# A selective-scan layer and a routed expert layer on one core: drives and scans by halves of a slot, states summed by accumulating transposes, and the gate by rows

## What is computed

```python
x_ssm, x_gate = split(x @ in_proj_w.T + in_proj_b)
x_conv = silu(conv1d(x_ssm) + conv_b)            # 4 taps, per channel
B, C   = split(x_conv @ bc_w.T + bc_b)           # 16 states each
dt     = softplus(x_conv @ dt_w.T + dt_b)
h = h * exp(dt * A) + dt * B * x_conv            # per channel and state, along the tokens
y = (sum over states of h * C + x_conv * D) * silu(x_gate)
out = y @ out_w.T + out_b + x                    # then the layer norm
```

## Time and profile before

| | |
|---|---|
| median of 3 runs | 1368.25 us (1363.77 to 1369.27) |
| the profiled execution | 1371.27 us |
| its span | 1369.4 us |
| stage 1, from the first drive to the last scan | 37.8 to 608.5 us |
| busy over the span | PE 85%, DVE 77%, ACT 66%, POOL 58% |

### The profile page before, as it was taken

The page is one execution under the profiler, slowest core; times in us unless marked ns, Lnnn a source line. Parts: engine busy times, 40 slices in busy tenths (PEclk is TensorE's granted clock), DMA queues, the critical chain, the costliest instruction groups (busy, mean ns, idle before and its releaser), DMA issues. The chain is left out here.

```text
span 1369.4 us, 18063 instructions
## 1 busy us (share of the span) xinstructions
PE 1168.3 (85%) x5138; PEld 802.5 (59%) x5138; DVE 1061.2 (77%) x1558; ACT 899.0 (66%) x1551; POOL 792.0 (58%) x566
## 2 busy tenths in 40 slices
PE   7879697988969797765799999999999999999940
PEld 3324252434334343324588888888888888888840
DVE  2999899999989999994777777777777777777744
ACT  4775849485856768425467777767767776767734
POOL 0457568888878888897643444444444444444342
PEclk9899999999999999887899999999999999999985
DMA  2543434545443545336676655566565655565537
GB/s 97 206 155 123 171 107 172 172 149 180 146 167 149 205 150 170 136 104 241 233 216 161 161 144 136 149 158 160 158 160 159 160 139 138 147 163 159 159 38 246
DMA packets 69258, 217.18 MB, mean 159 GB/s; under 512 B 7520, under 2 KB 43232, under 8 KB 56288
## 3 DMA queue, kind: packets, MB, share of 16 engines
q1 hardware_dynamic: 29664, 167.42, 34.0%
q0 software_dynamic: 26880, 36.72, 15.7%
q10 hardware_dynamic: 12672, 12.58, 2.8%
HBM read 165.54 MB, written 51.15 MB: 158 GB/s over the span
## 5 line engine op out<-in xcount | busy, mean ns | idle before, releaser
L641 PE MATMUL p_y<-read,small 128*128 128x512 f32 x512 | 260.4, 644 | 84.2 <-POOL read L1175 84.2
L1041 DVE TENSOR_TENSOR_SCAN state<-decay,p_bu 128x1024 f32<-128x1024 f32 x128 | 292.5, 2285 | 19.3 <-ACT decay L822 10.2
L1497 POOL DMA_INDIRECT total<-o_v,tok x144 | 266.0, 1847 | 45.4 <-issue 45.3
L641 PEld LDWEIGHTS p_y<-read,small 128*128 128x128 f32 x512 | 100.8, 205 | 226.9 <-POOL read L1175 123.3
L1495 POOL TENSOR_TENSOR scrap<-neg_half 128x1 f32<-128x1 f32 x36 | 13.0, 362 | 319.8 <-ACT o_v L1404 317.3
L822 ACT ACTIVATE decay<-dt,scan_rate 128x511 f32<-128x511 f32 x256 | 165.2, 713 | 20.6 <-DVE state L1041 20.2
L1175 POOL TENSOR_TENSOR read<-state,bc 128x1024 f32<-128x1024 f32 x64 | 150.2, 2353 | 34.5 <-DVE p_bu L1032 17.6
L505 ACT ACTIVATE gate_v<-p_g,bias 128x512 f32<-128x512 f32 x144 | 98.5, 684 | 103.0 <-PE p_up L495 96.8
L1217 POOL DMA_INDIRECT queues<-rows,index x128 | 134.4, 1050 | 31.7 <-issue 28.9
L1391 ACT ACTIVATE ah<-a_v 128x512 fp32r<-128x512 f32 x144 | 91.2, 633 | 93.0 <-DVE a_v L519 89.3
L1175 POOL TENSOR_TENSOR read<-state,first_wh 128x1024 f32<-128x1024 f32 x32 | 75.4, 2357 | 65.3 <-DVE p_bu L1032 51.7
(11 more groups left out here) (222 smaller groups left out, 3014.7 us busy)
## 6 DMA issues: line engine op xcount, KB each, us to landing
bc<-bc_rows SPq DMA_DIRECT2D x32, 1024.0 KB, 4.9
first_raw<-in_w_experts SPq DMA_DIRECT2D x19, 1668.0 KB
raw_w<-in_w_experts SPq DMA_DIRECT2D x18, 1668.0 KB
first_wh<-bc_rows SPq DMA_DIRECT2D x16, 1024.0 KB
first_wl<-bc_rows SPq DMA_DIRECT2D x16, 1024.0 KB
first_rows<-queues SPq DMA_DIRECT2D x19, 544.0 KB
xq<-queues SPq DMA_DIRECT2D x18, 544.0 KB
queues<-pad SPq DMA_DIRECT2D x9, 544.0 KB
```

Of the source, the lines that this page charges most:

```text
L641: mm = pe.matmul(p_y[h][:, :], ident[:, :], read[:, t % 4, h, :], start=False, stop=(t == SLOTS - 1))
L1041: dve.tensor_tensor_scan(flat(state[t % 4][:, :, :]), flat(decay[t % AHEAD][:, :, :]), p_bu[:, :], 0.0, ALU.mult, ALU.add).then_inc(s_stat ...
L1497: pool.indirect_dma_start(total, bass.IndirectOffsetOnAxis(ap=tok[t.p][:, a:a + 1], axis=0), o_v[t.p][:, a, :], None, compute_op=ALU.add). ...
```

## The change

1. **Halves.** Drive and scan of a slot become two instructions each, of 128x512. The order on DVE is drive(half 0), drive(half 1), what else the slot has, scan(half 0), scan(half 1). A half waits for its own half alone: the drive for the scan of the same half in the slot before, the scan for its drive and its decay. ACT and POOL wait for both halves, counted twice.
2. **Sums by transposes.** `sum_states` becomes 8 transposes of 128x128 (the product as stationary operand, the identity moving) that accumulate in `p_y`, so that `p_y` has tokens on its partitions. The start with `x_conv * D` becomes 8 matmuls of 128x128.
3. **The gate by rows.** `project_gate` makes the gate with tokens on the partitions: 8 products of 128x256 and 4 with the bias in three bf16 parts. The parts are made once, at the start (`spread_gate_bias`, `in_parts`). ACT copies without a bias.
4. **Turning back.** The gated `y_rows` is turned by 8 transposes (`turn_rows`, t = 3 on PE) into two new blocks of `p_bank`, which ACT copies into `y` (`take_turned`, first on ACT's list at t = 3). `project_out` waits for both copies.

```diff
-        return (["tr0", "tr1", "rt"] * d + ["in0", "in1"] * a + ["o0", "o1"] * c + ["cnt"] * d + ["cv0", "cv1"] * a
+        return (["tr0", "tr1", "rt"] * d + ["in0", "in1"] * a + ["yt0", "yt1", "o0", "o1"] * c + ["cnt"] * d + ["cv0", "cv1"] * a
...
+        def project_gate(r, b):
+
+            bank, done = block(r, f"in{HALVES + b}")
+            if r.like == Round.FIRST and b == 0:
+                pe.wait_ge(s_set_dve, 4)
+            for i in range(2):
+                to, at = bank[:, i * D:(i + 1) * D], (2 * b + i) * P
+                product(to, lambda k: xt[:, k, at:at + P], lambda k: w[:, k, IN + D:IN + 2 * D], stop=False)
+                mm = pe.matmul(to, ones[0:3, :], gate_parts[0:3, :], start=False, stop=True)
+            mm.then_inc(done, 1)
...
+            def of_rows(h, b):
+                return p_y[b // 2][:, b % 2 * D + h * P:b % 2 * D + (h + 1) * P]
+
             if t == 0:
                 after(pe, s_y, s.n)
                 for h in range(HALVES):
-                    pe.matmul(p_y[h][:, :], skip_w[:, h, :], xc[s.p][:, h, :], start=True, stop=False)
+                    for b in range(TT):
+                        pe.matmul(of_rows(h, b), xc[s.p][:, h, b * P:(b + 1) * P], skip_w[:, h, :],
+                                  start=(h == 0 and b % 2 == 0), stop=False, skip_group_check=True)
             pe.wait_ge(s_read, n + 1)
             for h in range(HALVES):
-                mm = pe.matmul(p_y[h][:, :], ident[:, :], read[:, t % 4, h, :], start=False, stop=(t == SLOTS - 1))
+                for b in range(TT):
+                    mm = pe.matmul(of_rows(h, b), read[:, t % 4, h, b * P:(b + 1) * P], ident[:, :], is_transpose=True,
+                                   start=False, stop=(t == SLOTS - 1), skip_group_check=True)
             mm.then_inc(s_added, 1)
+
+        def turn_rows(r, h):
+
+            bank, done = block(r, f"yt{h}")
+            if h == 0:
+                pe.wait_ge(s_y, r.s.at(-1).n + 1)
+            for b in range(TT):
+                mm = pe.transpose(bank[:, b * P:(b + 1) * P], y_rows[:, b, h * P:(h + 1) * P], ident[:, :])
+            mm.then_inc(done, 1)
 
         def project_out(r, b):
 
             bank, done = block(r, f"o{b}")
             s = r.s.at(-1)
-            if b == 0:
-                pe.wait_ge(s_y, s.n + 1)
+            for h in range(HALVES):
+                src, n = r.block(f"yt{h}")
+                pe.wait_ge(bank_read[src], n)
...
+        def take_turned(r, h):
+
+            bank, done = full(act, r, f"yt{h}")
+            act.activation(y[:, h, :], bank[:, :], ACT.Copy).then_inc(done, 1)
...
+        def weigh_inputs(s, t, h):
+
+            if t == 0 and h == 0:
                 dve.wait_ge(s_u, s.n + 1)
-            arrived(dve, s, t)
-            after(dve, s_state, SLOTS * s.n + t)
-            dve.tensor_tensor(p_bu[:, :].rearrange("p (a b) -> p a b", a=2), p_u[:, :].rearrange("p (a b) -> p a b", a=2),
-                              of_state(t, 0), ALU.mult).then_inc(s_bu, 1)
-
-        def scan(s, t):
-
-            n = SLOTS * s.n + t
-            dve.wait_ge(s_bu, n + 1)
-            dve.wait_ge(s_decay, 2 * n + 2)
-            after(dve, s_read, n - 3)
-            dve.tensor_tensor_scan(flat(state[t % 4][:, :, :]), flat(decay[t % AHEAD][:, :, :]), p_bu[:, :],
+            if h == 0:
+                arrived(dve, s, t)
+            after(dve, s_state, halves_done(s, t - 2) + h + 1)
+            dve.tensor_tensor(p_bu[:, h * LEN:(h + 1) * LEN], p_u[:, h * LEN:(h + 1) * LEN], row_of(t, 0), ALU.mult)\
+               .then_inc(s_bu, 1)
+
+        def scan(s, t, h):
+
+            dve.wait_ge(s_bu, halves_done(s, t - 1) + h + 1)
+            dve.wait_ge(s_decay, halves_done(s, t - 1) + h + 1)
+            if h == 0:
+                after(dve, s_read, SLOTS * s.n + t - 3)
+            dve.tensor_tensor_scan(state[t % 4][:, h, :], decay[t % AHEAD][:, h, :], p_bu[:, h * LEN:(h + 1) * LEN],
                                    0.0, ALU.mult, ALU.add).then_inc(s_state, 1)
...
             for h in range(HALVES):
-                last = dve.tensor_tensor(y[:, h, :], p_y[h][:, :], sg[s.p][:, h, :], ALU.mult)
+                last = dve.tensor_tensor(flat(y_rows[:, 2 * h:2 * h + 2, :]), p_y[h][:, :], sg[s.p][:, h, :], ALU.mult)
             last.then_inc(s_y, 1)
```

More of the change, by code:

```diff
@@ L264, in build @@
     y = sb("y", HALVES, LEN, at=one)
+    y_rows = sb("y_rows", TT, D, at=one)
+    gate_parts = sb("gate_parts", D, dt=BF16, at=one)
     z = sb("z", TT, D, at=one)
@@ L690, in count @@
             mm.then_inc(done, 1)
+        spread_gate_bias()
         for r in rounds(pe):
@@ L707, in pe_stage1 @@
                 if r.c and t == 3:
+                    turn_rows(r, 0)
+                    turn_rows(r, 1)
                     project_out(r, 0)
@@ L727, in pe_stage1 @@
                 if r.a and t in (10, 11):
-                    project(r, t - 8)
+                    project_gate(r, t - 10)
                 if t >= 2 and r.b:
@@ L761, in store_in @@
                 after(act, s_y, s.n - 1)
-            to = xpad[:, m, TAPS - 1:TAPS - 1 + LEN] if m < 2 else sg[s.p][:, m - 2, :]
-            act.activation(to, bank[:, :], ACT.Identity, bias=b_in[:, m:m + 1]).then_inc(done, 1)
+            if m < 2:
+                last = act.activation(xpad[:, m, TAPS - 1:TAPS - 1 + LEN], bank[:, :], ACT.Identity, bias=b_in[:, m:m + 1])
+            else:
+                last = act.activation(sg[s.p][:, m - 2, :], bank[:, :], ACT.Copy)
+            last.then_inc(done, 1)
         def store_conv(r, h):
@@ L816, in decays @@
         def decays(s, t):
-            after(act, s_state, SLOTS * s.n + t - AHEAD + 1)
+            after(act, s_state, halves_done(s, t - AHEAD))
             if t == 0:
@@ L879, in act_stage1 @@
             for t in range(SLOTS):
+                if r.c and t == 3:
+                    take_turned(r, 0)
+                    take_turned(r, 1)
                 if r.d and t == 3:
@@ L963, in dve_setup, with in_parts @@
         dve.tensor_reduce(b_bc2[:, :], b_bc[:, :], AX.X, ALU.add).then_inc(s_set_dve, 1)
+        def in_parts(to):
+            steps.then(dve.memset(to[:, :], 0.0))
+            for i in range(3):
+                steps.then(dve.tensor_copy(b_part[:, :], b_rest[:, :]))
+                if i < 2:
+                    steps.then(dve.tensor_tensor(b_rest[:, :], b_rest[:, :], b_part[:, :], ALU.subtract))
+                steps.then(dve.scalar_tensor_tensor(to[:, :], b_part[:, :], ident[:, i:i + 1], to[:, :], ALU.mult, ALU.add))
+        dve.wait_ge(s_gate_bias, 1)
+        steps.then(dve.tensor_copy(b_rest[:, :], p_bu[:, 0:D]))
+        in_parts(gate_parts)
         dve.wait_ge(s_const, SETUP)
         steps.then(dve.tensor_tensor(b_rest[:, :], b_out[:, :], ln_b[:, :], ALU.subtract))
[L967 to L973, removed]
+        in_parts(b_parts)
     def dve_setup_rest(dve):
@@ L1121, in dve_stage1 @@
                 if r.b:
-                    weigh_inputs(r, t)
+                    for h in range(HALVES):
+                        weigh_inputs(r.s, t, h)
                 if r.c and t == 2:
@@ L1162, in dve_stage1 @@
                 if r.b:
-                    scan(r.s, t)
+                    for h in range(HALVES):
+                        scan(r.s, t, h)
         return plan_steps
```

20 lines of the change are left out of this document (13 added, 7 removed).

## The result

The changed kernel takes 1360.5 us against 1366.6 for the kernel before (medians of ten runs each, taken on one chip): ratio 0.995, 95% interval 0.993 to 0.997, so 6.1 us less. The forecast was 1382; the time lies inside the range of 1357 to 1392, but on the other side of "no change".

A forecast was written before the change was run, and what follows sets the result against it. DVE was taken to set most slots' pace, closed by PE in slots 2 to 5 and ACT at slot 11. Rounds 2 to 6 +12.1, round 0 -1.8, round 1 -0.3, round 7 +1.0, tail +2.8: +13.8, 1382 us, range 1357 to 1392.

The forecast's parts named there:

- PE's clock in slots 0 to 2: Rounds 2 to 6, up to the second project: low clock makes PE's work 10.87 us, 1.8 later per round.
- row at 656.0: Profile row where the clock fell while 8 transposes ran, read as transposes not holding the clock as products do.
- Halves: DVE's plain slots: overlapping half instructions give 3.50 us, gaining 0.32 in the loop, 0.16 outside; 18.7 if nothing else bound.
- first rival: PE in the scan slots: transposes raise the clock like products; -4.6 us, 1364; chance 0.27.
- Slots 2 to 5: PE's closed stretch from lg to count: two sums -1.68, turning +1.90, so +0.22 us per round.
- Slot 11: DVE's scan waiting for ACT's decay: half decay saves 0.62, dt at low clock costs about 1.0; +0.4 us per round.
- Rounds 0 and 7: First and last rounds of stage 1: round 0 gains 1.8 us, round 7 loses 1.0.
- Tail: Chain from last gate to residual: turning adds 1.9 us, 2.8 at the low clock, and stage 2 starts later.
- Gate by rows: PE in slots 10 and 11 and set-up before the first drive: nothing; 3 us once if cover were gone.
- No overlap of halves: DVE's drives and scans: plain slots of 3.80 us, 1383 in all; chance 0.10.
- The base: Profiled execution took 1371.27 us against the median of 1368.25; the summed difference was applied to the median.
- second rival: PE's clock never matters: -1.6 us per round in rounds 2 to 6, -8.8 in all, 1360; chance 0.20.

The follow-up runs named there:

- zero transposes: Changed kernel plus 16 accumulating transposes of a tile of zeros into p_y ahead of each sum in slots 6 to 15, 0 and 1: 0.994 of before.
- halves alone: Kernel before with only drives and scans split in two, sums still products, nothing turned: 0.987 of before, 17.1 us less.
- rows alone: Changed kernel with whole drives and scans again, keeping sums by transposes, gate by rows and turning: 1.010 of before, 14.7 us more.
- count before out: Changed kernel with count products ahead of the output projection on PE, place and base in DVE's slot 4: 0.994 of before.
- zero products: Changed kernel plus two products of a tile of zeros into p_y ahead of each sum in slots 6 to 15, 0 and 1: 0.991 of before.

## Why the prediction was wrong, point by point

- **PE's clock in slots 0 to 2: the step that failed.** I took from the row at 656.0 that transposes don't hold the clock, and added 1.8 us to each of five rounds. In the forecast PE reaches the second `project` 10.87 us after sum(14); in after it takes 9.1, 8.9, 7.7, 9.7 and 9.1 in rounds 2 to 6 (round 4 before: 9.11). The low clock at the start was there, as forecast, but transposes alone raised it again. What it cost is the time by which the second `project` starts later behind lg than before's 0.23: nothing in rounds 2 and 5, 0.7 us in round 4, 1.4 in rounds 3 and 6, so 3.4 in all where the sum had 9. Slot 2, where lg waits for PE, grew by 0.4 in the five. The 656 row stood behind an idle time of 1.9 us, which I named as the doubt and gave 0.27. The Trainium skill, "TensorE: Matmul & The Clock Gate", Part 4, says full clock doesn't engage for transposes; the kernel with zero transposes held 1.00 over 12 us of transposes alone, so here the measurement decides against it.
- **Halves.** Mechanism right, size low. Forecast 3.50 for a plain slot, measured 3.42: the half scan follows after 1.12, not 1.15. From 2.22 to 1.12 is 1.10 saved for half of the columns, where the sum took half of 2.13. Filled slots gain too (slot 13: 4.66 to 4.55), where I had nothing. If nothing else bound, 3.42 and 0.12 for each of the 47 filled slots would give 31 us, an estimate, against the 18.7 of the forecast.
- **Luck in the first rival's number.** For rounds 2 to 6 it had -4.0 in all, and the table by round has -3.2 (the forecast +12.1). But it had -0.1 a round at slot 11, where the time grew by 7.4 in these rounds, and it didn't count the plain slots' 17.7 as coming through. Its mechanism for the clock is shown; its 1364 came near by errors that cancel.
- **Slots 2 to 5.** Turning 1.90 forecast, 1.87 measured. From lg to `count`'s last group it is 14.05 before and 14.94 after in round 4 (321.04 to 335.98); forecast +0.22, and the other 0.67 is the late second `project` of the first point. That `place` would wait 2 to 3 us was near: 0.9 to 2.5, 10.2 us in rounds 2 to 7. Without turning slot 5 loses 9.7.
- **Slot 11.** Cause right: dt begins at the low clock because shorter sums leave PE idle (forecast over 3 us, measured 4.16). The forecast was 1.0 us a round for the clock less 0.62 for the half decay, so 2 in five rounds; the slot grew by 7.0 us in all. 3.8 of it is the clock's, and 3.0 is already there with halves alone. DVE arriving earlier at ACT's chain fits that; it was not tested apart.
- **Rounds 0 and 7** gained 3.46 and 3.26, forecast 1.8 and a loss of 1.0. Round 7's slots have no projections behind them, and slot 11 there took back nothing. The second profile of before has 62.24 for round 7, so 1.2 of the 3.26 may be scatter.
- **Tail.** Forecast +2.8; +2.2 in the profile of after, 5.0 to 5.7 in the kernels with turning where the output projection began at the low clock (rows alone 23.4, count before out 23.6, zero products 23.1, zero transposes 23.0, against 17.9).
- **Gate by rows.** Forecast nothing for its set-up, and the first drive starts at 37.86 against 37.79. Its products weren't run apart from the rest of the rows layout.
- **No overlap of halves** is refuted by 3.42 against 3.80. I had quoted the Trainium skill, "VectorE: DVE Perf Modes", "The DRAIN you can't avoid", against the halves. The same section also says that a next operation that isn't held starts earlier; four instructions for two took 0.24 to 0.40 us less here, and by this the trace agrees.
- **The base.** The profile that I started from had a wait of `place` that isn't the kernel's, 5 to 6 us, and I mapped it onto a median. The sum adds differences and is free of it. (The second rival's terms, -8.8, give 1359 where I wrote 1360.)

## What to carry to other kernels

Where each instruction of an engine needs the result of the one before it, split both, so that each needs the one two back; splitting one alone gave 0.2% here at most. Work taken off an idle engine is no gain by itself. Where PE's idle time grew to 4.16 us here, its next products began at half the clock: look at what stands behind each idle stretch before you shorten a group. And judge the parts of a change one by one: here one part was worth 17 us and the other cost 15. Before you read a small difference between two profiles, profile the same kernel twice.

## What was not expected of the hardware

Accumulating fp32 transposes of 128x128 take 0.11 us each at full clock and count for the clock like products (0.99 against 0.99 over 552 us). The wait for a result of the instruction before is 0.19 to 0.20 us inside the loop and 0.04 outside it; with nothing waited for, loop slots and unrolled slots take the same 3.42. A wait of some 6 us was in the first profile of before and in the four kernels profiled together on one chip, and in none of the nine others; with it 27 us pass from the last residual to the last index, without it 21 to 22. In the kernel with 7446 instructions on PE the second pass of the loop loads instructions again (11 packets of q8 from 360 to 520 us, none there in after), and PE stands for 4.38 us at its start.
